# Writing the ones of four PSUM banks with four row tiles at once

## The chip, the cores and the metric

One core of a Trainium2 chip runs the whole kernel. The metric is the device time in microseconds. A core has five engines that run side by side and meet at semaphores: TensorE (PE, matrix products into the PSUM banks), VectorE (DVE), ScalarE (ACT), GpSimd (POOL), and SyncE (SP), which here issues DMAs.

## The reference

An input of shape (8, 64, 64, 64) passes two stages. The first is four scans, down, up, right and left, each step of which adds to a row the relu of a nine-tap convolution of the row before. The second is a linear attention with four heads of 32 channels:

```
xn = group_norm(x); q, k, v = split(w_qkv @ xn)
q = elu(q) + 1;  k = elu(k) + 1
k_sum = sum_n k;  kv = sum_n k v^T
out = (q @ kv) / (q @ k_sum + 1e-6)
out = group_norm(w_out @ out) + x
```

The change lies in the second stage, in the products that give q and k.

## The kernel before

The four scans come first (L533 on PE and the DVE lines around it) and last until about 440 us. The change doesn't touch them. The attention stage follows, one image after another, eight in all. Channels of one image fill 128 partitions as two groups of 64 (even and odd columns), and its 2048 positions are cut into four quarters of 512. For each quarter PE makes, in this order: `token_major` (L571, eight transposing products), `keys` (L579 and L585) into the banks `key_ps`, `queries` (L593 and L597) into the banks `query_ps`, and `gather` (L611, L615) for an earlier or the same quarter. Between these stand products of the image before: `small` (L622, L624, L638, L627), `denominators` (L650) and `output` (L661), the output of the image before and of the one before that. The order is written out by hand in PE's `iteration`, and the engines have the same order in theirs.

elu(z)+1 is taken as max(z+1, min(exp(z), 1)). The +1 is put in by PE: the first product into each key and query bank has a weight matrix that is zero but for one row of ones, and a moving matrix of ones, and so writes 1 everywhere. It takes 64 rows of the array, one bank in the upper half and one in the lower. The data products are added to it (L585, 24 products of 64 rows by 128 columns; L597, six of 64 rows by 512 columns). ACT takes the exponential of each bank with bias -1 (L1329 keys, L1335 queries), and DVE makes the rest (L968 keys, L978 queries), upon which `kp_ready` and `qp_ready` are raised and the bank is free. In the profile these products have the names `row_of_ones` and `first_rows`.

Around it: the denominators (L650) go to DVE (L1005, L1008 reciprocal), to DRAM and back over SP's queue (`bounce`), to POOL (L447), which multiplies the queries, and then to `output` on PE (L661). ACT copies the output (L1316) and applies the affine of the norm (L1349), DVE takes its statistics (L1019, L1013), and PE sums them over a group (L627).

Of the kernel before, what the change touches and what calls it, by code (L numbers as in the profile page):

```python
# [11 lines left out]
B, C, H, W = 8, 64, 64, 64  # L12
# [31 lines left out]
HEADS, DH = 4, 32  # L44
# [4 lines left out]
UNITS = 2 * NCHUNK  # L49
# [15 lines left out]
def columns(d):  # L65

    off = d - HALO
    return slice(max(0, -off), J - max(0, off)), slice(max(0, off), J + min(0, off))
# [16 lines left out]
def build(nc, x, k_td, k_dt, k_lr, k_rl, gn1_w, gn1_b, w_qkv, w_out, gn2_w, gn2_b, consts, out):  # L85
    with ExitStack() as ctx:
        def sb(name, shape, dt=F32):
            return ctx.enter_context(nc.sbuf_tensor(name, shape, dt))

        def sem(name):  # L90
            return ctx.enter_context(nc.semaphore(name))
# [20 lines left out]
        key_ps, tok_ps, acc_ps, query_ps, small_ps, out_ps = bank[0:2], bank[2], bank[3], bank[4:6], bank[6], bank[7]  # L112
        conv_rows = [[c[:, 0:GB * J].rearrange("p (b j) -> p b j", b=GB) for c in conv[g]] for g in range(GROUPS)]
        rows_of = slice(0, C), slice(C, P)
# [32 lines left out]
        row_of_ones = sb("row_of_ones", [P, 512], F16)  # L147
        first_rows = sb("first_rows", [P, P], F16)
# [38 lines left out]
        blanked, cleared = sem("blanked"), sem("cleared")  # L187
# [30 lines left out]
        query_done, query_exp, qp_ready = sem("query_done"), sem("query_exp"), sem("qp_ready")  # L218
# [18 lines left out]
        def at_least(eng, s, n):  # L237

            if not isinstance(n, int) or n > 0:
                eng.wait_ge(s, n)  # L240
# [171 lines left out]
        def _(pool):  # L412
# [8 lines left out]
            nc.gpsimd.memset(row_of_ones[:], 1.0)  # L421
            nc.gpsimd.memset(first_rows[:], 0.0).then_inc(cleared, 1)
            pool.wait_ge(cleared, 1)
            for d in range(2):
                nc.gpsimd.memset(first_rows[d * C:d * C + 1, :], 1.0).then_inc(cleared, 1)
            pool.wait_ge(cleared, 3)
            nc.gpsimd.memset(minus_one[:], -1.0)
            nc.gpsimd.memset(part[:], 1.0 / DH)
            nc.gpsimd.memset(half[:], -0.5).then_inc(zeroed, 1)
# [86 lines left out]
        def _(pe):  # L516

            for k in range(4):
                rows = (1, 64, 127, 190)[k]
                pe.wait_ge(w_high_ready[k], 1)  # L520
                with pe.Fori(0, STEPS - BODY + 1, BODY) as s:
                    for u in range(BODY):
                        for g in range(GROUPS):
                            pe.wait_ge(high_ready[g], s + (rows + u))
                            for part_n, (rows_16, ready, w) in enumerate(
# [5 lines left out]
                                for d in TAP_ORDER:  # L531
                                    to, of = columns(d)
                                    last = nc.tensor.matmul(conv_rows[g][u % SLOTS][:, :, to], w[:, k, d, :],  # L533
                                                            rows_16[:, u % SLOTS, g * GB:(g + 1) * GB, of],
                                                            start=part_n == 0 and d == HALO,
                                                            stop=part_n == 2 and d == TAP_ORDER[-1])
# [18 lines left out]
            def token_major(b, par, i):  # L555
# [16 lines left out]
                                             ident_16[:, :], start=n == k == 0, stop=k == 1, skip_group_check=True)  # L572
                t.then_inc(tok_done, 1)

            def keys(b, par, i):

                at_least(pe, kp_ready, KBANKS * b + 2 * i)
                for d in range(2):
                    nc.tensor.matmul(key_ps[d][:, :], first_rows[rows_of[d], :], row_of_ones[rows_of[d], :],  # L579
                                     start=True, stop=False)  # L580
                for n in range(4):
                    at = (4 * i + n) * P
                    for k, w in ((0, w_two_high), (0, w_two_low), (1, w_two_high)):
                        for d in range(2):
                            last = nc.tensor.matmul(key_ps[d][:, n * P:(n + 1) * P], split[rows_of[d], par, k, at:at + P],  # L585
                                                    w[rows_of[d], 1], start=False, stop=n == 3 and k == 1)
                            if n == 3 and k == 1:
                                last.then_inc(key_done, 1)

            def queries(b, par, i):  # L590
                at_least(pe, qp_ready, UNITS * b + 2 * i)
                for d in range(2):
                    nc.tensor.matmul(query_ps[d][:, :], first_rows[rows_of[d], :], row_of_ones[rows_of[d], :],  # L593
                                     start=True, stop=False)
                for k, w in ((0, w_two_high), (0, w_two_low), (1, w_two_high)):
                    for d in range(2):
                        last = nc.tensor.matmul(query_ps[d][:, :], w[rows_of[d], 0],  # L597
                                                split[rows_of[d], par, k, i * CHUNK:(i + 1) * CHUNK],
                                                start=False, stop=k == 1)
                        if k == 1:  # L600
                            last.then_inc(query_done, 1)
# [63 lines left out]
            def iteration(b, par, cur, prev, pp):  # L665
                for i in range(4):
                    if cur:
                        token_major(b, par, i)
                        keys(b, par, i)
# [8 lines left out]
                    if cur:  # L678
                        queries(b, par, i)
# [737 lines left out]
```

## Time and profile before

| what | value |
|---|---|
| time, median of 3 runs | 670.52 us (668.32 to 671.85) |
| profiled execution | 668.65 us, span 666.7 us |
| PE busy | 625.4 us (94%) |
| DVE busy | 567.6 us (85%) |
| ACT busy | 429.0 us (64%) |
| POOL busy | 127.5 us (19%) |
| mean granted clock of TensorE | 0.985 |

The times of the profile are of one execution. The span is the time between the first and the last instruction that it shows, and the rest of the 668.65 us lies around it. Busy shares are means over scans and attention together; the attention stage runs from about 440 us to the end.

### The profile page before, as it was taken

How to read it: one execution, taken by the hardware profiler on the slowest of the kernel's cores; microseconds unless marked ns; L12 is line 12 of the kernel's file. 1: busy time of each engine (PE TensorE's matmuls, PEld its weight loads, DVE VectorE, ACT ScalarE, POOL GpSimd, SP SyncE). 2: the span in 40 equal slices, each digit the busy share in tenths (PEclk: the TensorE clock that was granted, in tenths of full speed). 3: DMA queues.
4: the chain of work that ended last, by engine and by line, in shares of the span. 5: the costliest groups of instructions: out<-in, count | busy, mean ns of one | idle time of the engine just before them, and what ended most of it. 6: DMA issues, size and time to landing. Idle time of an engine off the chain costs nothing.

```text
span 666.7 us, 27877 instructions
## 1 busy us (share of the span) xinstructions
PE 625.4 (94%) x10516; PEld 537.7 (81%) x10516; DVE 567.6 (85%) x1953; ACT 429.0 (64%) x1062; POOL 127.5 (19%) x112
## 2 busy tenths in 40 slices
PE   4899999999999899999999999959989999999991
PEld 4899999999999899999999999955646656656550
DVE  4799989888898898989999999988968778878785
ACT  2565666577777766666666666657666867867744
POOL 0022200000000000000000000000053666667755
PEclk9999999999999999999999999979999999999997
DMA  9999970233333100000000000000326367468546
GB/s 177 205 204 197 178 149 0 58 78 76 81 75 77 47 1 0 0 0 0 0 2 0 0 0 0 0 1 1 73 69 147 74 133 171 101 128 185 112 87 126
DMA packets 72971, 50.29 MB, mean 75 GB/s; under 512 B 44064, under 2 KB 66016, under 8 KB 72928
## 3 DMA queue, kind: packets, MB, share of 16 engines
q1 hardware_dynamic: 69600, 48.91, 35.7%
q10 hardware_dynamic: 3328, 0.82, 0.6%
q8 instruction: 26, 0.43, 0.3%
q14 instruction: 17, 0.14, 0.1%
HBM read 32.34 MB, written 9.24 MB: 62 GB/s over the span
## 4 chain that ended last, share of the span: by engine, by line
PE 50%; DVE 30%; issue 11%; ACT 3%; DMA 2%; DVEq 2%; POOL 1%; ACTq 0%; SPq 0%; POOLq 0%
PE bank L533 34%; DVE scan_rows L821 7%; DVE parts L794 6%; DVE parts L821 6%; PE bank L661 3%; DVE fin L901 2%; PE bank L611 2%; DVE rows_h L978 2%; PE bank L597 2%; DVE stats L1019 2%; PE bank L585 1%; DVE kp L968 1%; PE bank L650 1%; PE bank L615 1%; PE bank L571 1%
## 5 line engine op out<-in xcount | busy, mean ns | idle before, releaser
L533 PE MATMUL bank<-parts 128*128 128x124 f16 (+2 forms) x7560 | 423.8, 219 | 15.6 <-DVE parts L260 8.4
L533 PEld LDWEIGHTS bank<-parts 128*128 128x128 f16 x7560 | 416.8, 98 | 22.4 <-issue 11.3
L1196 ACT ACTIVATE parts<-parts 128x128 f16<-128x128 f16 x506 | 156.6, 309 | 151.1 <-DVE parts L821 125.6
L794 DVE TENSOR_TENSOR parts<-scan_rows,parts 128x128 f16<-128x128 f32 x506 | 148.2, 293 | 14.2
L821 DVE SCALAR_TENSOR_TENSOR parts<-bank,cols_w 128x128 f16<-128x128 f32 x378 | 109.6, 290 | 20.6 <-PE bank L533 5.9
L821 DVE SCALAR_TENSOR_TENSOR scan_rows<-bank,cols_w 128x128 f32<-128x128 f32 x378 | 105.9, 280 | 0.1
L436 POOL TENSOR_TENSOR scale<-dev,half 128x2 f32<-128x2 f32 (+1 forms) x2 | 2.1, 1038 | 404.2 <-DVE dev L926 404.2
L447 POOL TENSOR_TENSOR rows_h<-rows_h 128x512 f32<-128x512 f32 x52 | 67.2, 1324 | 47.1 <-DMA rows_h<-bounce 47.1
L968 DVE SCALAR_TENSOR_TENSOR kp<-ex,bank 128x512 f32<-128x512 f32 x64 | 40.8, 679 | 22.6 <-ACT ex L1329 22.3
L1207 ACT ACTIVATE cols_w<-scan_rows 128x256 f32 x126 | 52.5, 417 | 5.7 <-issue 0.2
L1335 ACT ACTIVATE ex<-bank,minus_one 128x512 f32<-128x512 f32 x64 | 40.6, 690 | 14.8 <-PE bank L597 14.7
L978 DVE SCALAR_TENSOR_TENSOR rows_h<-ex,bank 128x512 f32<-128x512 f32 x64 | 41.0, 683 | 5.5 <-ACT ex L1335 4.8
L1329 ACT ACTIVATE ex<-bank,minus_one 128x512 f32<-128x512 f32 x64 | 40.7, 692 | 6.2 <-PE bank L585 5.9
L821 DVE SCALAR_TENSOR_TENSOR parts<-bank,rows_h 128x128 f16<-128x128 f32 x124 | 36.0, 290 | 8.7 <-issue 2.7
L611 PE MATMUL bank<-kp,tok 128*64 128x128 f32 x512 | 35.0, 279 | 0.2 <-DVE kp L968 0.2
L611 PEld LDWEIGHTS bank<-kp,tok 128*64 128x64 f32 x512 | 27.4, 136 | 9.3 <-issue 7.3
L821 DVE SCALAR_TENSOR_TENSOR scan_rows<-bank,rows_h 128x128 f32<-128x128 f32 x124 | 34.8, 280 | 0.0
L1223 ACT ACTIVATE cols_w<-ex 128x128 f32 (+1 forms) x84 | 34.0, 414 | 0.1
L1316 ACT ACTIVATE rows_h<-bank 128x512 f32<-128x512 f32 x26 | 15.6, 598 | 24.0 <-PE bank L661 22.6
L571 PEld LDWEIGHTS bank<-ident,parts 128*128 128x128 f16 x256 | 14.7, 99 | 19.7 <-issue 18.1
L901 DVE BATCH_NORM_STATS2 fin<-cols_w x96 | 28.7, 299 | 0.0
L1207 ACT ACTIVATE rows_h<-scan_rows 128x256 f32 (+1 forms) x64 | 26.6, 416 | 2.2
(144 smaller groups left out, 577.8 us busy)
## 6 DMA issues: line engine op xcount, KB each, us to landing
rows_h<-bounce SPq DMA_DIRECT2D x52, 256.0 KB, 4.8
cols_w<-x SPq DMA_DIRECT2D x12, 896.0 KB, 13.0
ex<-scan_rows SPq DMA_DIRECT2D x84, 64.0 KB, 2.0
out<-fin SPq DMA_DIRECT2D x10, 512.0 KB, 7.2
cols_w<-x SPq DMA_DIRECT2D x6, 640.0 KB, 10.7
kp<-scan_rows SPq DMA_DIRECT2D x40, 64.0 KB, 1.9
cols_w<-x SPq DMA_DIRECT2D x6, 256.0 KB, 6.1
out<-rows_h SPq DMA_DIRECT2D x12, 128.0 KB, 2.7
```

Source lines behind the costliest of these rows:

```text
L447: nc.gpsimd.tensor_tensor(qp[:, 1 - par, u, :], qp[:, 1 - par, u, :], recip_b[:, u, :], ALU.mult).then_inc(normed, 1)
L533: last = nc.tensor.matmul(conv_rows[g][u % SLOTS][:, :, to], w[:, k, d, :], rows_16[:, u % SLOTS, g * GB:(g + 1) * GB, of], start=part_n = ...
L611: nc.tensor.matmul(acc_ps[d * C:(d + 1) * C, 0:P], tok[:, i % 2, n * P + d * C:n * P + (d + 1) * C], kp[:, (2 * i + d) % 4, n * P:(n + 1) ...
L794: nc.vector.tensor_tensor(low[:, slot, gb, :], state[:, slot, gb, :] if row is None else row[:, gb, :], high[:, slot, gb, :], ALU.subtract ...
L821: nc.vector.scalar_tensor_tensor(out=to, in0=conv[g][u % SLOTS][:, 0:GB * J].rearrange("p (b j) -> p b j", b=GB), scalar=0.0, in1=add, op0 ...
L901: nc.vector.bn_stats(stats[:, b, bass.ds(n * 2 + (g - 2), 1), :].rearrange("p o s -> p (o s)"), cols[:, bass.ds(n * -BODY + (W + first), c ...
L968: nc.vector.scalar_tensor_tensor(out=kp[:, m % 4, :], in0=ex[:, m % 2, :], scalar=1.0, in1=key_ps[m % 2][:, :], op0=ALU.min, op1=ALU.max)\
L978: nc.vector.scalar_tensor_tensor(out=qp[:, par, u, :], in0=ex[:, 2 + u % 2, :], scalar=1.0, in1=query_ps[u % 2][:, :], op0=ALU.min, op1=AL ...
L1196: act.activation(high_down[:, slot, gb, :], high[:, slot, gb, :], ACT.Copy, scale=1.0 / LOW_SCALE).then_inc(down_ready[g], 1)
L1207: act.activation(to, state[:, slot, :, :], ACT.Copy).then_inc(saved, 1)
L1329: act.activation(ex[:, m % 2, :], key_ps[m % 2][:, :], ACT.Exp, bias=minus_one[:, :])\
L1335: act.activation(ex[:, 2 + u % 2, :], query_ps[u % 2][:, :], ACT.Exp, bias=minus_one[:, :])\
```

## The change

In quarters 0 and 1 of each image PE writes the ones of all four banks ahead of the keys, by four products that take 32 rows of the array each. The wait for the query banks moves with them, from ahead of the queries to ahead of the keys. In quarters 2 and 3 the ones are written where they were, two banks at a time, but also by products of 32 rows in place of 64. POOL sets four rows of ones in `first_rows`, one for each group of 32 partitions, where it set two.

```diff
-            for d in range(2):
-                nc.gpsimd.memset(first_rows[d * C:d * C + 1, :], 1.0).then_inc(cleared, 1)
-            pool.wait_ge(cleared, 3)
+            for d in range(4):
+                nc.gpsimd.memset(first_rows[d * DH:d * DH + 1, :], 1.0).then_inc(cleared, 1)
+            pool.wait_ge(cleared, 5)
...
+            def with_ones(banks, tiles):
+
+                for to, n in zip(banks, tiles):
+                    here = slice(n * DH, (n + 1) * DH)
+                    nc.tensor.matmul(to[:, :], first_rows[here, :], row_of_ones[here, :], start=True, stop=False)
+
             def keys(b, par, i):
 
                 at_least(pe, kp_ready, KBANKS * b + 2 * i)
-                for d in range(2):
-                    nc.tensor.matmul(key_ps[d][:, :], first_rows[rows_of[d], :], row_of_ones[rows_of[d], :],
-                                     start=True, stop=False)
+                if i < 2:
+                    at_least(pe, qp_ready, UNITS * b + 2 * i)
+                    with_ones((key_ps[0], query_ps[0], key_ps[1], query_ps[1]), range(4))
+                else:
+                    with_ones(key_ps, (0, 2))
...
             def queries(b, par, i):
-                at_least(pe, qp_ready, UNITS * b + 2 * i)
-                for d in range(2):
-                    nc.tensor.matmul(query_ps[d][:, :], first_rows[rows_of[d], :], row_of_ones[rows_of[d], :],
-                                     start=True, stop=False)
+                if i >= 2:
+                    at_least(pe, qp_ready, UNITS * b + 2 * i)
+                    with_ones(query_ps, (1, 3))
```

## Rows read from the trace of the kernel before

**Rows 1.** Stretch, us, busy PE, PEld, DVE, ACT, POOL, clock, DMA share, GB/s.

```profile
547.20:571.70 24.50, 24.35 (x359) 14.36 (x358) 19.48 (x36) 18.16 (x28) 15.81 (x12) 1.00 0.62 135
```

**Rows 2.** Timelines of POOL and PE, a steady image: start, duration (us).

```profile
565.53 5.05 POOL L447 TENSOR_TENSOR rows_h<-rows_h 128x512 f32<-128x512 f32 x4 [3.06 <-DMA rows_h<-bounce]
...
546.23 1.08 PE L661 MATMUL bank<-rows_h,mix 128*64 128x512 f32 x4
...
570.64 1.08 PE L661 MATMUL bank<-rows_h,mix 128*64 128x512 f32 x4
```

**Rows 3.** Timelines of PE (image 2, steady images) and DVE.

```profile
510.52 0.64 PE L615 MATMUL bank<-kp,ones 128*32 128x256 f32 x8
511.09 0.38 PE L627 MATMUL bank<-agg,cst 128*128 128x1 f32 x2
...
565.22 0.62 PE L571 MATMUL bank<-ident,parts 128*128 128x128 f16 x8
565.77 0.39 PE L579 MATMUL bank<-row_of_ones,first_rows 64*128 64x512 f16 x2
...
578.39 0.22 PE L585 MATMUL bank<-w_two_high,parts 64*128 64x128 f16 x2
578.45 0.38 PE L593 MATMUL bank<-row_of_ones,first_rows 64*128 64x512 f16 x2
578.66 0.38 PE L597 MATMUL bank<-parts,w_two_high 64*128 64x512 f16 x2
...
579.09 0.38 PE L597 MATMUL bank<-parts,w_two_high 64*128 64x512 f16 x2
579.40 1.09 PE L611 MATMUL bank<-kp,tok 128*64 128x128 f32 x16
...
583.66 0.64 PE L615 MATMUL bank<-kp,ones 128*32 128x256 f32 x8
584.45 0.38 PE L627 MATMUL bank<-agg,cst 128*128 128x1 f32 x2
...
584.13 0.26 DVE L1013 BATCH_NORM_AGGREGATE agg<-stats 128x2 f32<-128x24 f32 x1
```

**Rows 4.** Timeline of PE, image 0, quarters 0 and 1; idle before, releaser.

```profile
448.06 1.01 PE L571 MATMUL bank<-ident,parts 128*128 128x128 f16 x8 [3.63 <-DVE parts L1048]
...
452.30 0.62 PE L571 MATMUL bank<-ident,parts 128*128 128x128 f16 x8
452.99 0.39 PE L579 MATMUL bank<-row_of_ones,first_rows 64*128 64x512 f16 x2
...
455.37 0.39 PE L593 MATMUL bank<-row_of_ones,first_rows 64*128 64x512 f16 x2 [1.32 <-DVE rows_h L978]
```

**Rows 5.** Timeline of DVE, image 0, query products of quarter 0.

```profile
454.03 1.28 DVE L978 SCALAR_TENSOR_TENSOR rows_h<-ex,bank 128x512 f32<-128x512 f32 x2
```

**Rows 6.** The chain that ended last, in order of time, images 0 and 1.

```profile
466.86 1.28 DVE rows_h L978 x2
...
472.02 1.08 PE bank L650 x32
...
473.97 0.67 PE bank L585 x24
```

**Rows 7.** Timeline of PE, the last image.

```profile
636.55 1.17 PE L721 MATMUL bank<-recip,scan_rows 32*128 32x128 f32 x32
637.65 1.08 PE L727 MATMUL bank<-rows_h,mix 128*64 128x512 f32 x4
```

**Rows 8.** Waits of POOL: us in total, times, longest.

```profile
POOL parts L260 <- DMA yn<-L_conv_k_dt: 42.3, 1, 42.3
```

**Rows 9.** Timeline of PE, image 2, quarter 0.

```profile
495.12 1.08 PE L661 MATMUL bank<-rows_h,mix 128*64 128x512 f32 x4 [1.41 <-POOL rows_h L447]
```

**Rows 10.** PE's busy time and granted clock by microsecond.

```profile
441.00:442.00 1.00, 0.00 (x0) 0.88 0.00 0
451.00:452.00 1.00, 1.00 (x8) 0.50 0.00 0
```

## The prediction

> **What bounds the kernel now.** The change touches only the attention stage, the last third of the span, so I read that alone. First the page's shares: PE is busy 94% of the span (the table above). Then the busy time by image: in a steady image (547.2 to 571.7, one period) PE is busy 24.35 of 24.5 us [rows 1], which invites the thought that each 0.2 us taken from PE is gained. The timelines say it is not so. A steady image has two chains side by side. The first is PE's own stream. The second leaves PE with the last output product (L661 at 546.23), and goes over ACT (output copied, affine, exponentials), DVE (keys, queries, reciprocal of the second half), two DMAs through the bounce tensor and POOL's four products back to the next last output product: POOL ends 565.53+5.05 = 570.58, PE's L661 starts at 570.64 [rows 2]. In this chain PE does little, and it is as long as PE's stream. PE also waits twice inside an image for DVE: L579 starts 0.65 us after the transposes before it where 0.55 is its undisturbed spacing, and L627 waits for the aggregate (584.13+0.26) and starts 0.79 us after L615, where 0.57 is undisturbed, as in image 2 (510.52 to 511.09) [rows 3]. So PE has 0.32 us of slack from the last output product to L627, and none from L627 to the next one; there it can't gain, since POOL is 0.06 us ahead of it.
>
> The first image differs: PE waits for DVE there. It has L579 at 452.99 and its keys done at 454.05 (455.37-1.32), and then stands 1.32 us until DVE's two query products (454.03+1.28 = 455.31) free the query banks [rows 4, 5]. From 455.37 the chain that ended last runs on PE, then on ACT and at 466.86 on DVE, and from 472.02 on PE again, through the keys and queries of image 1's quarter 1 [rows 6].
>
> **What one edit costs on PE.** A pair of 512-column products in two row tiles takes 0.22 us (578.45, 578.66), so the two run side by side. A query pair directly behind the keys starts 0.06 us after their last pair (578.39, 578.45), the spacing of those pairs: no loss. Where the tile shape changes there is one: 64 rows to 128 costs 579.09 to 579.40 = 0.31, less 0.22, 0.09 us; 128 to 64 costs, with the eight transposes starting 0.057 us apart, 565.22+0.62-0.22+0.06 = 565.68 to 565.77, 0.09 us [rows 3]. From 32 rows to 128 (the last image's transposing back): the last of 32 starts at 636.55+1.17-0.27 = 637.45, its tile is free 4x0.029 later, L727 starts at 637.65: 0.08 us [rows 7]. The trace has no 32 to 64. Its bounds are 0 (64 rows are again a subset of the array, nothing need wait) and 0.19 (twice the switch, if the mode costs on leaving and on entering); I take s = 0.09, since three kinds of switch agree on it.
> The Trainium skill (TensorEngine Tiling, Key Properties) says that changing the tiling mode, and not just the tile, drains the engine. By that rule 32 to 64 costs like the others, the sum below; were it free, the time would be that of the second case below. No row here shows that pair of shapes, so the rule is untested by this trace.
> Four 32-row tiles: products in different row tiles start 0.028 us apart (24 of L585 in 0.67 us [rows 6]); between 0.22 (full overlap) and 0.22+2x0.028 = 0.27, I take 0.25. At the far end, no overlap beyond two, it is 0.43.
>
> By quarter, on PE:
> Quarters 0 and 1: the query pair goes (-0.22), four tiles in place of two (+0.03), a switch 32 to 64 is new (+0.09): -0.10 each. The queries still follow a 128-row product (L622 to L638), whose switch was there before.
> Quarter 2: the keys' ones get a 32 to 64 switch (+0.09); the query ones stood between keys and queries of one shape, and now cost 64 to 32 and 32 to 64 (+0.18): together +0.27.
> Quarter 3: keys +0.09, queries (128 before them as now) +0.09: +0.18.
> An image: +0.25 us, from seven new switches (0.63) less 0.38. So by these prices the change makes PE's stream longer.
> **The moved wait.** Keys of quarters 0 and 1 now wait for DVE's query products of the quarter before. Behind it stand keys, queries and gather, and behind these ACT and DVE. In steady images it is free: by the timelines DVE ends these products while PE is still at the output products ahead of the keys. In image 0, quarter 1, it is not: keys that ran up to 454.05 under the cover of DVE's work now start after 455.37 [rows 4, 5]. From there: four ones 0.25, switch 0.09, keys 0.67, queries 3x0.22 = 0.65, against ones 0.22 and queries 0.65: +0.79 us.
> POOL's two more memsets cost nothing: they lie at the start, and POOL then waits 42.3 us for a weight DMA [rows 8].
>
> **The sum.** Image 0, keys of quarter 0 at half clock, on the chain: two more tile starts and a switch, +0.2 (estimate: 2x2x0.028, and 0.09 to 0.14). Quarter 1 +0.79, quarter 2 +0.27, quarter 3 +0.18: 1.44 us when DVE takes over at 466.86. Image 1: the PE stretch from 472.02 holds a quarter 1, -0.10; its later quarters and quarter 0 of image 2 lie beneath PE's wait for POOL (1.41 us at 495.12 [rows 9]). Image 2 has no slack at L627: +0.27+0.18-0.10-0.10 = +0.25. Images 3 to 6: to L627 -0.10+0.27+0.09 = +0.26 against 0.32 of slack, 0; from there +0.09 (query ones of quarter 3) and -0.10: 0. Image 7: +0.02 and +0.09. Total 1.44-0.10+0.25+0.11 = +1.7 us. The profiled execution took 668.65 us (span 666.7), so 670.35; the median of the runs is 1.87 above it: 672.2.
> With s = 0 and 0.22 for four tiles: image 0 +0.67, image 1 -0.22, image 2 -0.22 (then POOL binds), the rest 0: +0.2. With s = 0.19: 0.3+0.89+0.57+0.38 = 2.1, image 2 +0.96, five images +0.65: +6.3.
>
> **Cases and chances.** One measurement of this kernel can't tell 0.5% (3.35 us) from no change.
> 1. As summed, +1.7: 672.2. Chance 0.45. Its own range is 670.5 to 673.8.
> 2. The switch 32 to 64 is free, +0.2: 670.7. Chance 0.12. For: the rows never show that pair. Against: every change of shape that they show costs 0.08 to 0.09.
> 3. Slower, by one mechanism: the new gap in image 0. PE stands idle from about 452.9 to 455.4, 2.5 us in place of 1.32, and the clock falls. The granted clock fell to half (1.2 GHz) within 441 to 442, in a stretch in which PE ran nothing, and it was last at half in 451 to 452, when PE had worked since 448.06, 3.9 us [rows 4, 10]. It decides if the clock falls in the gap: then 3.9 us of PE's time pass at half speed, which is 1.95 us of work lost: 674.1. Against: the 1.32 us idle was survived, and the fall needn't meet the gap. Chance 0.25.
> 4. The four tiles don't run side by side (the change doesn't do what it says): 0.43 for 0.25, +0.18 in each quarter 0 and 1. In image 0 0.18 and some 0.3 at half clock, 0.18 in image 1, 0.36 in image 2, in each later image 0.3: +2.5 more, 674.7. Against: 32 products of 128 columns in four row tiles start 0.029 us apart, where the transposes, in one tile, start 0.057 apart [rows 3, 7]. Chance 0.06.
> 5. The switch costs double, +6.3: 676.8. Chance 0.06.
> 6. Faster: PE's time is all that counts, and POOL's chain gives way with it. It decides only if switches are free and the DMAs of the bounce land earlier with PE: 16 pairs x 0.22 = -3.5, +0.67 for the new wait: -2.8, 667.7. Against: POOL ends only 0.06 us before L661 [rows 2]. Chance 0.06.
> The range goes from case 2, less 1.2 for the scatter of the runs (668.32 to 671.85), to between cases 4 and 5: 669.5 to 675.5. Slower by over 0.5% (above 673.9): half of case 3, case 5 and part of 4: 0.22. Faster by over 0.5%: half of case 6, and scatter: 0.05. Within: 0.73.
>
> **What would show it.** In the profile after: seven places per image where 32-row products are followed or preceded by 64-row ones, 0.31 us from a ones pair to the keys or queries behind it, in place of 0.22; in quarter 2 0.15 from the last key pair to the ones. Four ones within 0.1 us of each other, the keys 0.34 later. In image 0, quarter 1, L579's successor waiting about 2.4 us for DVE, and the keys behind it. The period of images 3 to 6 unchanged at 24.4 to 24.5 us, with PE's wait before L627 nearly gone. The prediction is wrong if that period moves by more than 0.1 us, if the clock falls near 455, or if image 0 gains back the wait by image 1.

## The result, and the profile after

The changed kernel takes 673.56 us in the median of 8 runs (671.56 to 675.21), the kernel before 670.43 us (668.05 to 671.85, 8 runs). The ratio is 1.0051, with a 95% interval of 1.0036 to 1.0066: slower by half a per cent, with an interval that leaves out 1. The profiled execution took 671.57 us, with a span of 669.5 us, where before they were 668.65 and 666.7.

PE's timeline of image 0, quarters 0 and 1, of the changed kernel (start, duration, idle before and its releaser); it answers to [rows 4]:

```profile
451.40 1.03 PE L571 MATMUL bank<-ident,parts 128*128 128x128 f16 x8
454.75 0.40 PE L579 MATMUL bank<-row_of_ones,first_rows 32*128 32x512 f16 x4 [2.32 <-DVE rows_h L985]
455.08 0.23 PE L593 MATMUL bank<-w_two_high,parts 64*128 64x128 f16 x2
...
455.76 0.38 PE L604 MATMUL bank<-parts,w_two_high 64*128 64x512 f16 x2
455.98 0.51 PE L604 MATMUL bank<-parts,w_two_low 64*128 64x512 f16 x2
456.28 0.63 PE L604 MATMUL bank<-parts,w_two_high 64*128 64x512 f16 x2
456.85 1.97 PE L618 MATMUL bank<-kp,tok 128*64 128x128 f32 x16
```

The moved wait is there: PE stands 2.32 us for DVE's query products, and the keys (L593), which ran ahead of this wait before, run behind it. The durations tell a second story. The query pairs have 0.38 us at first and 0.63 us at the end, and the gather (L618) takes 1.97 us where undisturbed it takes 1.09. The granted clock says why (PE's busy time and clock by stretch, changed kernel); it answers to [rows 10], for the stretch behind the gap:

```profile
453.00:456.00 3.00, 1.25 (x32) 1.00 0.00 0
456.00:457.00 1.00, 1.00 (x8) 0.55 0.00 0
457.00:459.00 2.00, 2.00 (x20) 0.50 0.00 0
459.00:460.00 1.00, 1.00 (x14) 0.75 0.00 0
```

The clock had risen to 2.4 GHz before 453, and falls to 1.2 GHz a second time just behind the gap, for about 3.4 us of full work.

The steady images, PE's timeline of the changed kernel, answering to [rows 3]:

```profile
580.71 0.22 PE L593 MATMUL bank<-w_two_high,parts 64*128 64x128 f16 x2
580.87 0.39 PE L579 MATMUL bank<-row_of_ones,first_rows 32*128 32x512 f16 x2
581.19 0.39 PE L604 MATMUL bank<-parts,w_two_high 64*128 64x512 f16 x2
581.41 0.38 PE L604 MATMUL bank<-parts,w_two_low 64*128 64x512 f16 x2
...
586.20 0.64 PE L622 MATMUL bank<-kp,ones 128*32 128x256 f32 x8
586.77 0.38 PE L634 MATMUL bank<-agg,cst 128*128 128x1 f32 x2
```

From the last key pair to the ones it is 0.16 us where it was 0.06, and from the ones to the queries 0.32 where it was 0.21: a change between 64 and 32 rows costs 0.10 us in either direction. And L634 starts 0.57 us behind L622, undisturbed, where before it was 0.79: PE's slack at the group sum has been used up. The other wait inside the image is gone too; before, the transposes and ones of quarter 3 were 0.65 us apart,

```profile
581.00 0.62 PE L571 MATMUL bank<-ident,parts 128*128 128x128 f16 x8
581.65 0.39 PE L579 MATMUL bank<-row_of_ones,first_rows 64*128 64x512 f16 x2
```

and in the changed kernel they are 0.56 us apart (583.53 and 584.09), where 0.55 is undisturbed.

Where the time went, by image, from PE's timelines (us; the first column is the start of image 1's transposes less that of image 0's; the second the start of quarter 1 of image 2, less the start of image 1; the third from there to quarter 1 of image 7, five periods; the last the whole from image 0's transposes to PE's last product):

| kernel | image 0 | to image 2, quarter 1 | five periods | all |
|---|---|---|---|---|
| before | 19.84 | 30.70 | 122.07 | 206.92 |
| before, second profile | 19.85 | 31.35 | 122.07 | 207.59 |
| changed | 22.66 | 30.14 | 122.97 | 210.30 |
| changed, second profile | 22.51 | 30.89 | 122.96 | 210.87 |

Image 0 takes 2.7 to 2.8 us more, five periods take 0.9 us more, and the stretch between, which hangs on the two DMAs through the bounce tensor, scatters by half a microsecond either way in one and the same kernel.

### The profile page after: what moved, and what is told of

The parts are those of the page before. It is cut to its first block, busy times and chain, and to the rows that moved or that the text cites. A ratio compares the mean times of both kernels' runs of the same rounds, so it can differ in the third digit from the quotient of the medians.

```text
span 669.5 us, 27894 instructions
## 1 busy us (share of the span) xinstructions
PE 628.6 (94%) x10516; PEld 535.7 (80%) x10516; DVE 569.3 (85%) x1953; ACT 428.7 (64%) x1062; POOL 128.5 (19%) x114
## 4 chain that ended last, share of the span: by engine, by line
PE 57%; DVE 25%; issue 8%; DMA 4%; DVEq 1%; ACT 1%; POOL 1%; SPq 1%; ACTq 0%; POOLq 0%
PE bank L533 31%; DVE scan_rows L828 7%; DVE parts L801 6%; DVE parts L828 6%; PE bank L618 4%; PE bank L593 3%; PE bank L668 3%; PE bank L604 3%; DMA cols_w<-x 3%; DVE fin L908 2%; PE bank L622 2%; PE bank L571 2%; PE bank L579 2%; PE bank L657 2%; DMA rows_h<-bounce 1%
## 5 line engine op out<-in xcount | busy, mean ns | idle before, releaser
L618 PE MATMUL bank<-kp,tok 128*64 128x128 f32 x512 | 35.8, 283 | 0.0
L618 PEld LDWEIGHTS bank<-kp,tok 128*64 128x64 f32 x512 | 28.1, 139 | 9.5 <-issue 7.7
```

Of the source, the lines that this page charges most:

```text
L618: nc.tensor.matmul(acc_ps[d * C:(d + 1) * C, 0:P], tok[:, i % 2, n * P + d * C:n * P + (d + 1) * C], kp[:, (2 * i + d) % 4, n * P:(n + 1) ...
```

## The experiments

All ratios are against the kernel before, run on the same chip. The clock is the mean granted clock over the executions of that kernel; that of the kernel before is 0.9855 to 0.986, that of the changed one 0.9812. This mean takes in the end of the kernel as well, where the profiles show another 9 to 13 us at half clock, nearly all of it behind PE's last product, where it costs nothing. So it is a weak witness for image 0 (0.983 for the second profile of the kernel before, 0.984 for that of the changed kernel, which has the fall), and the clock by stretch is what the argument rests on. The diffs are cut: helper functions and the words around them are left out.

**The moved wait alone.**

```diff
 at_least(pe, kp_ready, KBANKS * b + 2 * i)
+if i < 2:
+    at_least(pe, qp_ready, UNITS * b + 2 * i)      # ones stay 64-row products
...
-at_least(pe, qp_ready, UNITS * b + 2 * i)
+if i >= 2:
+    at_least(pe, qp_ready, UNITS * b + 2 * i)      # ahead of the queries
```

> The kernel before with one edit: in quarters 0 and 1 the wait for the query banks stands ahead of the keys. All ones stay 64-row products. Theory (the moved wait and the clock carry most of the loss): image 0, quarter 1 starts its keys behind DVE's query products, +0.89 us (keys 0.67 and their ones 0.22 out of cover), PE stands idle 2.3 to 2.5 us there, the granted clock falls to half right after and costs 1.3 to 2 us more; +2.2 to 2.9 us in all, 672.6 to 673.3, and no other place changes. Rival (the tile shapes carry it): only +0.9 us or less, the clock stays up, 671.3. In the profile: clock 1.00 or 0.50 in the three microseconds behind the gap.

Measured: 672.69 us, ratio 1.0032 (1.0013 to 1.0051), clock 0.9834. Image 0 took 22.44 us, 2.60 more than before, and the gap was 2.33 us:

```profile
455.95 0.39 PE L581 MATMUL bank<-row_of_ones,first_rows 64*128 64x512 f16 x2 [2.33 <-DVE rows_h L981]
```

```profile
454.00:456.00 2.00, 0.05 (x2) 1.00 0.00 0
456.00:458.00 2.00, 2.00 (x30) 0.58 0.00 0
```

(the first from PE's timeline, the second PE's clock by stretch). No tile shape is changed here, and image 0 loses nearly what it loses in the changed kernel (2.82 and 2.66 us in its two profiles), with the same fall of the clock. So most of the loss of image 0 is the wait and what comes with it.

**Image 0, quarter 1 as before, all else changed.**

```diff
-if i < 2:
+if i < 2 and not (b == 0 and i == 1):
     at_least(pe, qp_ready, UNITS * b + 2 * i)
     with_ones((key_ps[0], query_ps[0], key_ps[1], query_ps[1]), range(4))
```

> The changed kernel, but image 0 quarter 1 writes its ones as quarters 2 and 3 do: keys first, then the wait and the query ones. Theory: the gap before 455 shrinks to about 1.3 us behind keys that run under cover, the clock doesn't fall; what stays are the switches of tile shape, 0.75 us in image 0 and 0.3 to 0.5 us behind it: +1.0 to +1.3 us against the kernel before, 671.5 to 671.8. Rival (the switches carry the loss): within 0.7 us of the changed kernel, 673 or above.

Measured: 671.94 us, ratio 1.0023 (1.0007 to 1.0039). Image 0 took 20.32 us, +0.48 in place of +2.82; behind the gap, now 1.22 us, the clock stayed at 1.00. The 0.48 us are what the rest of the change costs in image 0 without the moved wait. The five periods keep their loss and more (124.33 us; image 4 has a slow POOL instruction, told of below).

**The gap filled.**

```diff
 if i < 2:
+    if b == 0 and i == 1:
+        for _ in range(38):
+            nc.tensor.matmul(out_ps[:, 0:P], ident_16[:, :], ident_16[:, :], start=True, stop=True)
     at_least(pe, qp_ready, UNITS * b + 2 * i)
```

> The changed kernel with 38 extra 128-column products of the identity into a bank that is free then, ahead of the wait in image 0 quarter 1. They fill the gap and compute nothing that is read. Theory: the clock falls because PE stands idle there; filled, it stays at 1.00, the moved wait keeps its own +0.79 us: 1.2 to 1.6 us faster than the changed kernel, about 672.2. Rival (the fall isn't due to the gap, or costs nothing): the clock still falls behind 455, or the time stays at 673.6.

Measured: 672.79 us, ratio 1.0029 (1.0019 to 1.0040), clock 0.9858. The timeline and the clock of PE:

```profile
452.06 0.62 PE L571 MATMUL bank<-ident,parts 128*128 128x128 f16 x8
453.45 2.29 PE L587 MATMUL bank<-ident 128*128 128x128 f16 x38 [0.77 <-DVE kp L978]
455.83 0.40 PE L579 MATMUL bank<-row_of_ones,first_rows 32*128 32x512 f16 x4
```

```profile
452.00:455.00 3.00, 2.23 (x38) 1.00 0.00 0
455.00:457.00 2.00, 1.91 (x44) 1.00 0.00 0
```

Image 0 took 20.99 us: +1.15, against +2.82 in the changed kernel. The work that counts is the same and the wait is kept. From the ones of quarter 1 to the start of image 1 it took 13.57 us (455.83 to 469.40), in the changed kernel 15.14 (454.75 to 469.89): 1.57 of the 1.67 us between the two lie behind the gap, where the clock differs, and the other 0.10 ahead of it. So the fall of the clock costs about 1.6 us. The ratios differ by 0.0022 or 1.5 us; their intervals just overlap, so by themselves they would not show it. The profile of this kernel also has the slow POOL instruction told of below (124.67 us in the five periods).

**The four tiles alone, without the narrow ones of quarters 2 and 3.**

```diff
-    with_ones(key_ps, (0, 2))       # quarters 2 and 3
+    ones_64(key_ps)                 # two 64-row products, as before
...
-    with_ones(query_ps, (1, 3))
+    ones_64(query_ps)
```

> The changed kernel, but quarters 2 and 3 write their ones by 64-row products as before; quarters 0 and 1 keep the four tiles. Theory: an image's PE stream is 0.20 us shorter than before in place of 0.25 longer, yet images 3 to 6 keep their period of 24.4 to 24.6 us, since POOL's chain sets it; image 0 keeps its wait and the fall of the clock: +1.6 to +2.2 us against before, 672.0 to 672.6. Rival (PE's stream sets the period): images 3 to 6 each 0.2 us shorter than before, 24.2 to 24.3 us, and 671 or below.

Measured: 674.02 us, ratio 1.0056 (1.0038 to 1.0074), clock 0.9815. The five periods took 122.14 us, as before (122.07) and not 121.1: PE's stream is 0.2 us shorter per image and nothing comes of it. That the whole is no faster than the changed kernel was against my number by 1.5 us. In its profile image 0 took 23.24 us, and the clock had not even risen ahead of the gap (PE's clock by stretch):

```profile
448.00:453.00 5.00, 4.99 (x50) 0.50 0.01 3
453.00:455.50 2.50, 0.21 (x2) 0.50 0.00 0
455.50:460.00 4.50, 4.47 (x46) 0.50 0.00 0
```

Here half clock lasted from about 443.7 to 460.8. That accounts for the profile; that it is what makes the median of the six runs is argued from their clock of 0.981 to 0.982, not shown.

**The narrow shape alone,** nine new switches per image and nothing saved.

```diff
-nc.tensor.matmul(key_ps[d][:, :], first_rows[rows_of[d], :], ...)      # 64 rows
+with_ones(key_ps, (0, 2))                                              # 32 rows, all quarters
...
+with_ones(query_ps, (1, 3))
```

> The kernel before in its order and with its waits, but all ones are written by 32-row products, two at a time. Nine new switches of tile shape per image and nothing saved, so the price of the switches alone. Theory: 0.09 to 0.10 us each, 0.85 us of PE time per image, which POOL's chain and the 0.3 us of slack at the output's group sums no longer cover: images 3 to 6 take 0.4 to 0.5 us more than 24.5, the whole +3.5 to +4.5 us, 674 to 675. Rival (PE isn't what sets the period, switches are hidden too): periods of 24.5 us, +1 us or less.

Measured: 673.11 us, ratio 1.0033 (1.0013 to 1.0052). The transposes that open images 5 and 6, in PE's timeline:

```profile
567.84 0.62 PE L571 MATMUL bank<-ident,parts 128*128 128x128 f16 x8
...
592.89 0.62 PE L571 MATMUL bank<-ident,parts 128*128 128x128 f16 x8
```

The period is 25.05 us, where before it was 24.4 to 24.5: of the 0.9 us that nine switches at 0.10 cost on PE, some 0.55 are seen and the rest is slack. The total, 2.3 us above the kernel before, came out 1.2 us below the low end of what I had expected.

**No query ones at all,** 0.87 us less PE time per image.

```diff
-for d in range(2):
-    nc.tensor.matmul(query_ps[d][:, :], first_rows[rows_of[d], :], row_of_ones[rows_of[d], :], start=True, stop=False)
...
-start=False, stop=k == 1)
+start=k == 0 and w is w_two_high, stop=k == 1)
```

> The kernel before without the 64 products that write the ones of the query banks; the first data product clears the bank, so the queries lack their +1. It takes 0.22 us per quarter off PE, 0.87 us per image, with no new switch and no moved wait. Theory: POOL's chain, which PE hardly touches, sets the period, so images 3 to 6 keep 24.4 to 24.5 us and what is gained is gained in images 0 and 2 and at the end: -0.5 to -1.5 us, 669 to 670. Rival (PE's stream sets the period): 23.6 to 23.8 us per image and -5 to -7 us, 664 to 665.

Measured: 669.87 us, ratio 0.9977 (0.9957 to 0.9997). The same transposes:

```profile
567.49 0.62 PE L571 MATMUL bank<-ident,parts 128*128 128x128 f16 x8
...
591.71 0.62 PE L571 MATMUL bank<-ident,parts 128*128 128x128 f16 x8
```

A period of 24.22 us, where the same image took 24.43 before: 0.87 us taken off PE's stream gives 0.2 us. That is neither my "unchanged" nor the rival's 23.6 to 23.8, and far nearer the first. It bounds what the change could ever have given in a steady image, since it removes only half as much.

**The four tiles without either cost** (both edits above together).

```diff
-if i < 2:
+if i < 2 and not (b == 0 and i == 1):
...
-    with_ones(key_ps, (0, 2))
+    ones_64(key_ps)
-    with_ones(query_ps, (1, 3))
+    ones_64(query_ps)
```

> The changed kernel without both of its costs: quarters 2 and 3 have 64-row ones as before, and image 0 quarter 1 writes its query ones behind its keys. What stays of the change are the four tiles in quarters 0 and 1 (15 of 16 times), 0.10 us less PE time each, and in image 0 quarter 1 the query ones as 64-row products. Theory: the same time as before within 0.5 us (670.4), since the steady period isn't PE's. Rival: the four tiles have another cost of their own, +1 us or more.

Measured: 671.45 us, ratio 1.0008 (0.9989 to 1.0027). Image 0 took 19.97 us, 0.13 more than before. The idea of the change, freed of both its costs, changes nothing that can be measured.

**A warm clock for the kernel before,** products that nothing reads, between the scans and image 0.

```diff
+def fill(n):
+    for _ in range(n):
+        nc.tensor.matmul(query_ps[0][:, :], first_rows[:, :], row_of_ones[:, :], start=True, stop=True)
+for g in range(GROUPS):
+    pe.wait_ge(row_ready[g], 254)
+fill(10)
...
-for n in range(2):
+for n, count in ((0, 2), (1, 15)):
     image_mean(n, FIRST, small_ps, stat_ready, stat_done)
+    fill(count)
```

> The kernel before with 27 products of 512 columns that nothing reads, in PE's idle time between the last scan step and the first image's first transposes, to keep the clock up. Theory: the clock stays at 1.00 through 440 to 453; transposes, keys and queries of image 0 quarter 0 take 2.1 us less of PE time, of which 1.2 us are on the chain to DVE's first key product: -1.0 to -1.3 us, about 669.2. Rival (DVE's chain sets that stretch, or the fillers delay the first image): within 0.4 us of the kernel before.

Measured: 668.95 us, ratio 0.9976 (0.9953 to 0.9999), clock 0.9911. PE's timeline:

```profile
445.75 3.40 PE L549 MATMUL bank<-row_of_ones,first_rows 128*128 128x512 f16 x15
449.52 0.61 PE L580 MATMUL bank<-ident,parts 128*128 128x128 f16 x8 [0.37 <-DVE parts L1057]
...
451.91 0.62 PE L580 MATMUL bank<-ident,parts 128*128 128x128 f16 x8
```

Quarter 0 takes 2.39 us on PE in place of 4.24 [rows 4], and image 0 18.61 us in place of 19.84.

> warm_before once more, with more rounds, as the candidate that may beat both kernels. Theory: ratio 0.9976 to the kernel before was no accident, 0.997 to 0.9985. Rival: 1.000 within the interval.

Measured: 668.29 us, ratio 0.9981 (0.9970 to 0.9993). It beats both kernels, by 1.3 us the kernel before. In this profile the clock did fall, for 3.4 us behind the gap of 1.32 us that image 0 has in any case, and image 0 took 20.20 us. In the first warm profile the same gap left the clock at 1.00 and image 0 took 18.61 us. That is one kernel with and without the fall, and the difference, 1.59 us, is the price of it once more. A gap that the clock survives in one execution is no safe one.

**A warm clock for the changed kernel.**

```diff
+fill(10), fill(2), fill(15) as in the last one, and the 38 products in the gap
```

> The changed kernel with products that nothing reads both between the scans and the first image (27 of 512 columns) and in the gap of image 0 quarter 1 (38 of 128 columns). Theory: the granted clock stays at 1.00 from 438 to 470; what is left of the change against warm_before is the moved wait and the switches, +1.5 to +2.2 us: 670.5 to 671.2. Rival (the clock was not what cost the change its last part): 672 or above.

Measured: 670.37 us, ratio 1.0017 (1.0002 to 1.0032) to the kernel before, that is 0.0036 or 2.4 us above the warm version of the kernel before. The clock stayed at 1.00 up to 470:

```profile
440.00:448.00 8.00, 7.34 (x40) 1.00 0.01 2
448.00:454.00 6.00, 5.02 (x88) 1.00 0.00 0
454.00:460.00 6.00, 6.00 (x106) 1.00 0.01 3
```

Image 0 took 19.76 us against 18.61, so wait and switches cost 1.15 us there, the number that the filled gap gave.

**Both kernels profiled once more.**

> The kernel before, profiled once more, for what differs from one execution to the next. Half clock ahead of image 0 for 6.8 or 10.2 us; POOL's L462 of image 4 0.34 or 1.35 us; image 1 start 19.8 us after image 0's, within 0.5.

Measured: 668.50 us in one run, half clock for 10.2 us ahead of and in image 0, image 0 19.85 us, L462 of image 4 0.34 us.

> The changed kernel, profiled once more. Theory: again a gap of 2.3 to 2.5 us on PE in image 0 quarter 1 and half clock behind it (or half clock that isn't left before it), image 1 start 2.3 to 3.4 us later behind image 0's than in the kernel before.

Measured: 672.45 us in one run. The gap was 2.90 us, more than expected (PE's transposes ahead of it ran at full clock and ended earlier), the clock fell to 0.50 behind it, and image 0 took 22.51 us, 2.66 more than in the kernel before.

## Why the prediction was right, and where it was off

The time lay within the range, on the edge between what a measurement can tell and what it can't, and most steps of the sum hold. The number itself was 1.4 us too low, and the main step behind it is the choice between cases 1 and 3. Of the three signs that the prediction named for being wrong, two came: the clock fell near 455, and the period of images 3 to 6 moved by more than 0.1 us in two of the four in either pair of profiles. The third did not: image 0 gained nothing back. That the clock alone seems to fill the whole difference is in part luck. Image 2 and images 3 to 6 together lost 0.65 us more than forecast, and the stretch from image 1 to image 2, quarter 1, came out some 0.5 us shorter than before in both pairs of profiles, where 0.1 was forecast and the scatter is as large.

- **The clock (case 3).** I gave it a chance of 0.25 and added it to nothing. It came in every profile that has the long gap and a clock that had risen ahead of it: both of the changed kernel and that of the moved wait alone. Whether the eight timed runs all have it is not shown; their mean clock of 0.9812, 0.004 below that of before, fits. That the gap causes the fall is shown by filling it and by shortening it to 1.22 us, both of which left the clock at 1.00. Its price was forecast as 1.95 us, measured about 1.6. With it the sum would have given 674.1, a shade above the 673.56 measured.
- **The moved wait.** Forecast +0.79 us in image 0 with a gap of 2.4 us; the gap was 2.32, and 2.90 in the second profile. The 0.79 was not measured by itself. With the clock held behind the gap (filled gap), wait and switches cost image 0 1.15 us up to the start of image 1. The sum had 1.44 us for them at the end of the last query product of image 0, and a wait of PE for DVE in the kernel before takes up 0.2 of it, which leaves 1.24:

```profile
466.31 1.09 PE L611 MATMUL bank<-kp,tok 128*64 128x128 f32 x16 [0.20 <-DVE kp L968]
```

- **The price of a switch.** Forecast 0.09 us for 32 to 64 rows, a pair of shapes that no row of before showed; measured 0.10, into the narrow shape and out of it. The Trainium skill (TensorEngine Tiling (Array Packing), Key Properties) says that a changed tiling mode drains the engine; the trace agrees that such a change costs time, with 0.32 us from a pair of ones to the queries behind it where 0.21 is undisturbed. Case 2 is refuted, and so is case 5.
- **Four tiles side by side.** Forecast 0.25 us for four and 0.34 to the keys behind them; measured 454.75 to 455.08, 0.33. Case 4 is refuted.
- **Image 2.** Forecast +0.25 us, measured 24.62 less 24.12 = +0.50, the same in both pairs of profiles. The forecast had +0.35 up to the start of image 3; it took 18.11 us against 17.70, +0.41, as its six new switches at 0.10 in place of 0.09 make it. From there to quarter 1 the forecast had -0.10, for the four tiles of quarter 0, and this step failed: 6.51 us against 6.42, +0.09. PE's timelines, before and changed:

```profile
519.67 1.08 PE L661 MATMUL bank<-rows_h,mix 128*64 128x512 f32 x4
520.68 1.08 PE L650 MATMUL bank<-rows_h,den_w 128*32 128x128 f32 x32
521.71 1.08 PE L661 MATMUL bank<-rows_h,mix 128*64 128x512 f32 x4
...
521.42 1.08 PE L668 MATMUL bank<-rows_h,mix 128*64 128x512 f32 x4
522.63 1.08 PE L657 MATMUL bank<-rows_h,den_w 128*32 128x128 f32 x32
523.64 1.08 PE L668 MATMUL bank<-rows_h,mix 128*64 128x512 f32 x4
```

  The first output does come 0.09 us earlier behind the start of the image (3.28 us against 3.37). But the denominators need DVE's masked sums (L986, L993 in the changed kernel), and these hang on the keys, which the four tiles and the switch delay: they end 4.35 us behind the start of the image against 4.23. So L657 starts 1.21 us behind the output ahead of it, where 1.01 is undisturbed. The last output follows 1.01 us behind the denominators, the undisturbed spacing, so here PE's own stream sets it and not POOL.
- **POOL.** In image 2 its products take 5.94 us in the changed kernel, against 5.39 before. The timelines of POOL and DVE, before and changed:

```profile
516.27 5.39 POOL L447 TENSOR_TENSOR rows_h<-rows_h 128x512 f32<-128x512 f32 x4 [3.22 <-DMA rows_h<-bounce]
514.47 2.35 DVE L284 TENSOR_TENSOR parts<-yn,parts 128x1024 f16<-128x1024 f32 x2
...
517.56 5.94 POOL L447 TENSOR_TENSOR rows_h<-rows_h 128x512 f32<-128x512 f32 x4 [3.29 <-DMA rows_h<-bounce]
516.32 2.35 DVE L284 TENSOR_TENSOR parts<-yn,parts 128x1024 f16<-128x1024 f32 x2
```

  This is no second loss: they end 5.36 us behind the start of image 3 in both kernels. And it shows what the second chain hangs on. In images 2 to 6 of the two profiles of the kernel before there are ten such meetings, and in all of them the products end 4.83 to 4.85 us behind the end of DVE's L284, whether they start 0.19 or 1.17 us ahead of that end (four products that meet no L284 take 4.98 us). So in the steady images it is DVE's L284, and not the landing of the bounce DMA, that sets when POOL is done. DVE comes to L284 behind the query products of quarter 3. Before they start it waits for ACT's exponentials (0.50 us in image 4), and ACT for PE's queries (1.30 us), so this chain leaves PE at the queries of quarter 3. That L284 holds POOL up is read from these times; no run varied it.
- **Images 3 to 6.** Forecast 0. Measured 0.19, 0.20, 0.00 and 0.01 us, in the second profile 0.10, 0.21, 0.11 and -0.03: 0.4 in all. The cause is that of image 2. Up to the start of the next image PE's own stream is 0.41 us longer, against 0.31 us of slack: 18.11 us in place of 18.00. Behind it the -0.10 of quarter 0 comes in two of the four in the first profile (6.40 us against 6.52 in images 6 and 7) and in one in the second. In the others the denominators' wait for DVE, 0.1 or 0.2 us, or that of the last output for POOL takes it. Between L627 and the last output product, where the query ones of quarter 3 add their switch, it is 10.71 us in both kernels in the image of the excerpt above (584.45 to 595.16, 586.77 to 597.48).
- **That PE's time isn't what counts (case 6).** Held, with a correction. Four tiles alone leave the period as it was, and a quarter of the time saved without query ones comes through. Time added to PE comes through to more than half (some 0.55 of 0.9 us). PE's stream and the chain over DVE and POOL are of about the same length, so a loss shows and a gain hardly does. But the second chain is not one that PE leaves alone: it passes through DVE's query products, masked sums and L284, which hang on PE's keys and queries of the same image.

What stays open: 124.33 us in the five periods of the kernel with a late image 0 and 123.51 in that with the moved wait alone go with POOL's slow instruction (below), and the stretch through the bounce DMAs scatters by 0.5 us in one kernel; neither was taken apart.

## What to carry to other kernels

Count the changes of tile shape that an edit makes, not only the products that it removes: here each cost 0.10 us, and seven of them ate up two pairs of 0.22. When a wait is moved ahead of work that used to run under its cover, look at how long the engine will stand idle and whether TensorE's clock survives it, in the granted clock of the same trace; the clock cost here about 1.6 us, more than the wait and the switches of image 0 together (1.15 us). And where two chains of equal length run side by side, work taken off one of them is worth little, while work added to it is paid.

## What the runs showed of the hardware

- Half clock that sets in ahead of image 0 lasted 6.8 us in three profiles without filling products ahead of image 0, 10.2 us in seven, and 17 us in one, where it ran on through the gap. The mean clock of one execution of the kernel before goes from 0.981 to 0.988. 27 products that nobody reads, in time in which PE is idle, are worth 1.3 us.
- A gap of 1.32 us on PE left the clock at 1.00 in [rows 4]. Gaps of 0.68 and 1.32 us, one shortly after the other, left it at 1.00 in the first warm profile of the kernel before and were followed by 3.4 us at half clock in the second. Gaps of 2.32, 2.33 and 2.90 us were followed by it in all three profiles in which the clock had risen ahead of them.
- POOL's products (128x512, f32) took longer beside DVE's L284 (128x1024, f32 to f16): a run of four took 4.98 us by itself, 5.39 when it started 0.55 us ahead of L284's end, and 5.90 when it started 1.06 us ahead of it.
- A POOL instruction on a single column (L462) took 0.34 us, but 1.33 to 1.39 us in five of fourteen profiles, once each, four of them in image 4, and that image came out longer. POOL's timeline, the moved wait alone:

```profile
550.96 0.29 POOL L455 TENSOR_SCALAR scale<-scale,norm 128x1 f32<-128x1 f32 x1 [0.21 <-POOL scale L451]
551.46 1.34 POOL L462 TENSOR_SCALAR shift<-dev,scale,norm 128x1 f32<-128x1 f32 x1 [0.21 <-POOL scale L455]
```

  What delays it was not tried.
